# Weights made in three stages a step apart, large transfers on ScalarE's queue, two banks for p6, x's high parts on ScalarE, the opening's sums on GpSimd

## Time and profile before

| | us |
|---|---|
| median of the runs | 2794.37 |
| profiled execution, its own time | 2791.71 |
| its span, first to last instruction | 2789.9 |
| TensorE busy | 2471.3 (89%) |
| VectorE busy | 1668.8 (60%) |
| ScalarE busy | 975.5 (35%) |
| GpSimd busy | 402.0 (14%) |

### The profile page before, as it was taken

One profiled execution on the slowest core, in us unless ns is written; L12 is line 12 of the kernel. 1 busy time (PEld: TensorE's weight loads), 2 busy tenths in 40 slices (PEclk: granted clock), 3 DMA queues, 4 the chain that ended last, 5 costly groups with the idle time before them and its releaser, 6 DMA issues. The chain is left out here.

```text
span 2789.9 us, 30463 instructions
## 1 busy us (share of the span) xinstructions
PE 2471.3 (89%) x11214; PEld 1119.0 (40%) x11214; DVE 1668.8 (60%) x2827; ACT 975.5 (35%) x1247; POOL 402.0 (14%) x296
## 2 busy tenths in 40 slices
PE   2669879787787888999999999999899999999999
PEld 1324334333332333444444444444344444444444
DVE  7676667765676676577878878765543252241341
ACT  6575556544454454444454444111000000001001
POOL 1020101111222221111111111111101001001011
PEclk8789999988898998999999999999999999999999
DMA  6445454545445444855566555431776777686774
GB/s 226 155 147 159 146 187 157 182 137 176 157 165 176 158 167 145 321 196 185 192 211 212 200 177 193 144 107 71 291 317 256 307 274 299 260 323 265 282 311 153
DMA packets 172993, 571.15 MB, mean 205 GB/s; under 512 B 23632, under 2 KB 48896, under 8 KB 155052
## 3 DMA queue, kind: packets, MB, share of 16 engines
q1 hardware_dynamic: 163484, 535.11, 53.1%
q10 hardware_dynamic: 9360, 34.08, 3.9%
HBM read 380.38 MB, written 188.75 MB: 204 GB/s over the span
## 5 line engine op out<-in xcount | busy, mean ns | idle before, releaser
L1512 PE MATMUL ps<-arena 128*128 128x512 f16 x7200 | 1621.8, 388 | 169.5 <-DVE arena L1116 86.5
L1512 PEld LDWEIGHTS ps<-arena 128*128 128x128 f16 x7200 | 715.4, 100 | 1063.4 <-issue 171.7
L1631 PE MATMUL ps<-arena 128*128 128x512 f16 x3696 | 800.4, 380 | 10.4 <-DVE arena L1320 10.4
L822 ACT ACTIVATE arena<-arena,bias_t 128x1024 f32<-128x1024 f32 (+1 forms) x520 | 574.2, 1141 | 33.9 <-DMA arena<-in_dn 13.8
L1631 PEld LDWEIGHTS ps<-arena 128*128 128x128 f16 x3696 | 362.1, 98 | 448.7 <-issue 14.2
L1154 DVE CAST arena<-arena 128x512 f16<-128x512 f32 x364 | 204.6, 574 | 211.7 <-POOL arena L777 71.7
L1157 DVE TENSOR_TENSOR arena<-arena 128x512 f16<-128x512 f32 x364 | 297.3, 829 | 0.0
L767 POOL TENSOR_TENSOR arena<-arena 128x512 f32<-128x512 f32 x52 | 78.3, 1507 | 1138.5 <-DVE arena L1288 952.7
L837 ACT ACTIVATE arena<-arena 128x512 f16<-128x512 f32 x147 | 86.3, 622 | 339.8 <-DVE arena L1084 132.1
L888 ACT ACTIVATE arena<-ps,gate_back 128x512 f32<-128x512 f32 x84 | 57.4, 683 | 381.4 <-PE ps L1512 381.2
L787 POOL TENSOR_TENSOR arena<-arena 128x512 f32<-128x512 f32 x64 | 84.3, 1326 | 699.8 <-DMA arena<-in_xt 574.2
(11 more groups left out here) (106 smaller groups left out, 1245.9 us busy)
## 6 DMA issues: line engine op xcount, KB each, us to landing
isc<-arena SPq DMA_DIRECT2D x308, 256.0 KB, 2.0
arena<-wdsc SPq DMA_DIRECT2D x28, 2816.0 KB, 9.8
arena<-isc SPq DMA_DIRECT2D x28, 2816.0 KB, 16.8
arena<-xnsc SPq DMA_DIRECT2D x48, 1024.0 KB, 16.6
wsc<-arena SPq DMA_DIRECT2D x21, 1792.0 KB, 7.5
arena<-wsc SPq DMA_DIRECT2D x42, 768.0 KB, 5.2
arena<-in_gu ACTq DMA_DIRECT2D x43, 512.0 KB, 4.1
wdsc<-arena SPq DMA_DIRECT2D x77, 256.0 KB, 2.1
```

The source lines that it names most:

```text
L822: a_.activation(buf, src, ACT.Prelu, bias=bias_t[:, i:i + 1], scale=scale, alpha=alpha).then_inc(ramps, 1)
L1512: ins = t_.matmul(ps[:, bank, :], wreg[:, b, w, wa, k, :], xreg[:, j, o, k, xa, :], start=start and (k, wa, xa) == (0, 0, 0), stop=stop an ...
L1631: ins = t_.matmul(ps[:, bank, :], ring_w[b][:, k, wa, g, :], ring_i[b][:, k, xa, :], start=first and (k, wa, xa) == (0, 0, 0), stop=r not ...
```

## The change

- **Weights in three stages.** For weight u + 1: items 0 to 3 in step (u - 1, 1), items 4, 5, 6, 7, 9 in step (u, 0), items 8, 10, 11, 12 in step (u, 1). ScalarE's w_high are grouped as [0, 4, 5] and [1, 3, 6, 2], right behind p1_copy. Of the ramps 10 are in step (u, 0) and 6 in step (u, 1), half ahead of sil_a and half behind it.
- **Queues.** store_w, load_w, load_xb and load_ring are issued by ScalarE, the loads by `reloads` at the start of its step (one after sil_a).
- **Banks.** From step 23 on p6 alternates between banks 6 and 7. The first products of the closing phase wait for their own bank.
- **x jobs.** ScalarE makes the high parts (`x_high`), VectorE only the low parts.
- **Opening.** GpSimd makes all four sums of each early block. The layer norm of tiles 0 to 7 and of tiles 8 to 15 is one group each, with three applies of each on GpSimd; that of 8 to 15 is in slot 3 of step 0, its transposes behind step 0's products, and its evacuations alternate with w_high of weight 1. The later norms are in slot 3, not 5. The first weight and block order on VectorE changes with it.
- **Half tile LAST.** It uses operands 0 and 1 of its buffer, not 2 and 3.

The core of the diff (inner code is shown with less indentation):

```diff
 NEARLY = 8
...
+W_AT[0] = [(1, i) for i in range(13)]
+W_AT[2] = [(2, i) for i in range(4)]
+W_AT[3] = [(2, i) for i in (4, 5, 6, 7, 9, 8, 10, 11, 12)] + [(3, i) for i in range(4)]
 for _s in range(4, 40):
     _u, _j = PASS[_s]
-    W_AT[_s] = (_u + 1, 0, 6) if _j == 0 else (_u + 1, 6, 13)
-RAMP_AT = {0: (1, 4, 16), 1: (2, 0, 12), 2: (2, 12, 16), 3: (3, 0, 16)}
+    if _j == 0:
+        W_AT[_s] = [(_u + 1, i) for i in (4, 5, 6, 7, 9)]
+    else:
+        W_AT[_s] = [(_u + 1, i) for i in (8, 10, 11, 12)] + [(_u + 2, i) for i in range(4) if _u + 2 < LAST or i == 0]
+W_AT[40] = [(LAST, 6)]
+STORE_W_AT = {0: 1, 3: 2, 40: LAST}
+STORE_W_AT.update({_s: PASS[_s][0] + 1 for _s in range(4, 40) if PASS[_s][1]})
+RAMP_AT = {0: (1, 4, 16), 1: (2, 0, 8), 2: (2, 8, 16), 3: (3, 0, 16)}
 for _s in range(4, 40):
     _u, _j = PASS[_s]
     if _u + 2 < NU:
-        RAMP_AT[_s] = (_u + 2, 8 * _j, 8 * _j + 8)
+        RAMP_AT[_s] = (_u + 2, 0, 10) if _j == 0 else (_u + 2, 10, 16)
 NDOWN = 11
 for _i in range(4):
     RAMP_AT[40 + _i] = (NU, 4 * _i, 4 * _i + 4)
...
+W_CUT = {5: [0, 0, 0, 1, 2, 3, 5], 8: [0, 0, 0, 1, 2, 3, 8], 13: [0, 0, 0, 0, 0, 0, 13], 4: [0, 0, 0, 0, 0, 0, 4],
+         9: [0, 0, 0, 0, 0, 0, 9], 1: [0, 0, 0, 1, 1, 1, 1], 0: [0] * 7}
+W_CUT[9], W_CUT[5], W_CUT[6] = [0, 0, 2, 3, 4, 5, 9], [0, 0, 1, 2, 3, 4, 5], [0, 0, 1, 2, 3, 4, 6]
+def p6_bank(s):
+    return 6 if s < 23 else 6 + s % 2
+def p6_before(s):
+    return next((t for t in range(s - 1, -1, -1) if p6_bank(t) == p6_bank(s)), None)
...
         g.tensor_tensor(early_t[:, 1, :], b[:, 0, 1, :], b[:, 0, 0, :], ALU.subtract).then_inc(ep_made, 1)
+        pool.wait_ge(ep_made, 4 * e + 1)
+        g.tensor_tensor(early_t[:, 2, :], b[:, 1, 1, :], early_t[:, 1, :], ALU.subtract).then_inc(ep_made, 1)
+        if e:
+            pool.wait_ge(e_lo, 5 * e - 1)
+        pool.wait_ge(ep_made, 4 * e + 2)
+        g.tensor_tensor(early_t[:, 0, :], b[:, 1, 0, :], early_t[:, 2, :], ALU.subtract).then_inc(ep_made, 1)
         if e:
             pool.wait_ge(e_lo, 5 * e)
         g.tensor_tensor(early_t[:, 3, :], b[:, 1, 1, :], b[:, 0, 1, :], ALU.subtract).then_inc(ep_made, 1)
+    def lnorm_share(tiles):
+        pool.wait_ge(ln_out, tiles[0] // 8 + 1)
+        for tt in tiles:
+            g.tensor_scalar(nat[nat_slot(tt)], nat[nat_slot(tt)], mv[:, tt % 8, 0:1], y[:, 1, tt % 8:tt % 8 + 1],
+                            ALU.subtract, ALU.mult).then_inc(xn_done, 1)
     def sums(c):
...
+        early_sums(e)
+    lnorm_share([13, 14, 15])
+    for e in range(4, NEARLY):
         early_sums(e)
     for c in JOBS:
         sums(c)
...
+    def store_w(u):
+        act.wait_ge(w_lo, w_base(u + 1, 7, 1))
+        b = wbuf(0, u)
+        if u == LAST:
+            act.dma_start(wsc[u, :, 0:2, :, :], wflat[:, b, 0:2, :, :]).then_inc(wst[u % 2], 16)
+        else:
+            act.dma_start(wsc[u, :, :, :, :], wflat[:, b, :, :, :]).then_inc(wst[u % 2], 16)
...
+    def load_w_first(u):
+        load_w(u, 0, 1)
+        load_w(u, 4, 7)
+    def load_w_second(u):
+        load_w(u, 1, 2)
+        load_w(u, 2, 4)
...
+    def reloads(s):
+        h, u, j = STEPS[s]
+        if h == 0:
+            if s == 41:
+                act.wait_ge(prod, prod_at(40, "p5"))
+                load_xb(0, 5)
+                load_xb(0, 6)
+                act.wait_ge(prod, prod_at(39, "p3"))
+                load_w(0, 4, 7)
+                load_w(0, 2, 4)
+            elif s == 42:
+                act.wait_ge(prod, prod_at(41, "r"))
+                act.wait_ge(prod, prod_at(40, "p3"))
+                for o in (0, 4, 2, 3):
+                    load_xb(0, o)
+            elif s == 43:
+                act.wait_ge(prod, prod_at(42, "p5"))
+                load_w_first(1)
+                act.wait_ge(prod, prod_at(41, "p2"))
...
+                load_xb(1, o)
+        elif s == NSTEP + 1:
+            act.wait_ge(prod, prod_at(43, "p2"))
+            load_w(0, 1, 2)
+            load_xb(1, 1)
+        elif s == NSTEP + 3:
+            act.wait_ge(prod, prod_at(s - 1, "p5"))
+            load_w_first(2)
+        elif s == NSTEP + 4:
+            act.wait_ge(prod, prod_at(s - 2, "p3"))
+            load_w_second(2)
+            act.wait_ge(prod, prod_at(s - 1, "p5"))
+            load_w_first(3)
+        elif s == NSTEP + 5:
+            act.wait_ge(prod, prod_at(s - 2, "p3"))
+            load_w_second(3)
+        elif u == 20 or u == LAST:
+            if (u, j) == (LAST, 1):
+                act.wait_ge(prod, prod_at(s - 2, "p2"))
+                load_ring(0)
+        elif u >= 3 and j == 0:
+            act.wait_ge(prod, prod_at(s - 1, "p5"))
+            load_w_first(u + 1)
+        elif u >= 3 and j == 1:
+            act.wait_ge(prod, prod_at(s - 2, "p3"))
+            load_w_second(u + 1)
...
+    def x_high(c, o):
+        if made_before(c, o):
+            act.wait_ge(t_made, 4 * JOB[c] + made_before(c, o))
+        else:
+            act.wait_ge(blk_in, 32 * x_number(c) + 32)
+        n = STAGED[c + (o,)]
+        if n >= NSLOT:
+            act.wait_ge(st_out[n % NSLOT], 16 * (n // NSLOT))
+        a_.activation(dest(c, o)[:, 0, :], operand_of(c, o), ACT.Copy).then_inc(x_hi, 1)
...
-    for s in range(TOTAL + 1):
+    store_w(0)
+    def ramps_of(s, a, b):
+        w, first, end = RAMP_AT.get(s, (0, 0, 0))
+        for n in range(first + (end - first) * a // 4, first + (end - first) * b // 4):
+            ramp(w, n)
+    p1_copy(0)
+    ramps_of(0, 0, 4)
+    for at, ops in ((8, [0]), (10, [4, 5]), (12, [1, 3]), (14, [6, 2])):
+        for tt in (at, at + 1):
+            for hh in (0, 1):
+                evac(tt, hh)
+        for o in ops:
+            w_high(1, o)
+    for e in EARLY_AT[0]:
+        for g in range(5):
+            early_high(e, g)
+    for s in range(1, TOTAL + 1):
+        h, u, j = STEPS[min(s, TOTAL - 1)]
+        if s < TOTAL:
+            reloads(s)
         if s >= 2:
             sil_b(s - 2)
         if half_tile_at(s - 1, "p3"):
             evac(*half_tile_at(s - 1, "p3"))
         if s < TOTAL:
             p1_copy(s)
-        if s == 0:
-            for tt in range(8, 12):
-                for hh in (0, 1):
-                    evac(tt, hh)
-        h, u, j = STEPS[min(s, TOTAL - 1)]
-        wu, w0, w1 = W_AT.get(s, (None, 0, 0))
-        ru, r0, r1 = RAMP_AT.get(s, (None, 0, 0))
-        if 4 <= s < 40 and wu != LAST:
-            for o in ([0], [1, 3])[j]:
-                w_high(wu, o)
+        if 4 <= s < 40 and u + 1 != LAST:
+            for o in ([0, 4, 5], [1, 3, 6, 2])[j]:
+                w_high(u + 1, o)
+        if s in XJOB_AT:
+            for o in (0, 1, 2):
+                x_high(("x",) + XJOB_AT[s], o)
         if half_tile_at(s, "p6"):
             evac(*half_tile_at(s, "p6"))
-        for n in range(r0, r0 + (r1 - r0) // 4):
-            ramp(ru, n)
-        if s == 0:
-            for tt in range(12, 16):
-                for hh in (0, 1):
-                    evac(tt, hh)
+        ramps_of(s, 0, 2)
+        if s in XJOB_AT:
+            for o in (4, 5):
+                x_high(("x",) + XJOB_AT[s], o)
         if half_tile_at(s, "p5"):
             evac(*half_tile_at(s, "p5"))
-        if s:
-            sil_a(s - 1)
+        sil_a(s - 1)
+        if s == 40:
+            w_high_last()
+        elif s == 43:
+            act.wait_ge(prod, prod_at(43, "r"))
+            load_w(0, 0, 1)
+        elif s == NSTEP + 40:
+            load_w(LAST, 0, 1)
+            load_w(LAST, 1, 2)
         if half_tile_at(s, "p2"):
             evac(*half_tile_at(s, "p2"))
...
+                x_high(("x",) + XJOB_AT[s], o)
+        for e in EARLY_AT.get(s, ()):
+            for g in range(5):
+                early_high(e, g)
+        if s == 3:
             for o in W_ORDER:
-                w_high(wu, o)
-        if s == 0:
...
         tp, r = i // 7, i % 7
+        if i == 0:
+            act.wait_ge(prod, len(PRODS))
+        if i + 1 < 28:
+            load_ring(i + 1)
...
-    def lnorm(tiles):
+    def lnorm(tiles, mine):
         m = len(tiles)
+        if tiles[0] >= 8 and m == 8 or tiles[0] == 16:
...
-        for i, tt in enumerate(tiles):
+            if k < 2 or m < 8:
+                step(v_.tensor_tensor(r, r, t, ALU.mult))
+            else:
+                v_.tensor_tensor(r, r, t, ALU.mult).then_inc(ln_out, 1)
+                dve.wait_ge(ln_out, tiles[0] // 8 + 1)
+        for i, tt in enumerate(tiles[:mine]):
             v_.tensor_scalar(nat[nat_slot(tt)], nat[nat_slot(tt)], mv[:, i, 0:1], y[:, 1, i:i + 1],
                              ALU.subtract, ALU.mult).then_inc(xn_done, 1)
...
+                return
             if made_before(c, o):
                 dve.wait_ge(t_made, 4 * JOB[c] + made_before(c, o))
-            elif c[0] == "x":
-                dve.wait_ge(blk_in, 32 * x_number(c) + 32)
             else:
                 s = step_of(c[2] // 2, 2 * c[1] + 1, c[2] % 2)
                 dve.wait_ge(ib_made, s + 1)
```

(56 more changed lines are left out.)

261 lines of the change are left out of this document (76 added, 185 removed).

## The result

The changed kernel takes 2672.18 us (median of 4 runs, 2668.99 to 2672.88) against 2796.60 for the kernel before on the same chip (4 runs): a ratio of 0.9552, 95% interval 0.9535 to 0.9568. The profiled execution spans 2671.1 us at a granted clock of 0.967. The forecast was 2597, so 119 us of span were gained where 196 were expected.

The account below looks back on a forecast made before the run. TensorE bounds the kernel, idling where VectorE is late, notably steps 23 to 38. Gains 87 + 56 + 15 + 38 = 196 take the span from 2789.9 to 2594, time 2597; range 2565 to 2635, wide range 2540 to 2675.

Parts of the forecast that it names:

- (a): Both long stretches: half the gain, as x_high's way is paid in full and bursts hold staging slots; 2668 us, chance 0.16.
- (d): Weights: three stages don't work, w_high still waits for VectorE; casts, norm, opening and queues alone pay; 2656 us, chance 0.12.
- Opening, minus 15 forecast: To the end of step 4: sums and applies move from VectorE to GpSimd, first products end sooner; minus 15 us.
- Steps 7 to 22, minus 56: Later tiles' layer norm: moved to slot 3, it shortens the stall in every fourth step; 386.8 becomes 331, minus 56 us.
- cycle of 82.7: Steps 7 to 22: four steps take 18.1 + 26.6 + 18.1 + 20.0 = 82.7 us, four times.
- Steps 23 to 38, minus 87: Where x's blocks are split: three weight stages and x's highs on ScalarE relieve VectorE; 424.3 becomes 337, minus 87 us.
- x's highs: Steps 23 to 38: seven casts in each of 8 steps leave VectorE, 28 us; new waits of 18 and 8.
- the second block 5 late, four times, 20: Steps 23 to 38: VectorE's wait for each pair's second block, behind the first job's last low and four scale loads.
- balance for VectorE before (421.5 of 424.3): Steps 23 to 38, kernel before: VectorE's busy time plus three waits nearly fills the stretch, so VectorE is the bound.
- Steps 41 to 45, minus 12: Transfers on ScalarE's queue: w_high_last no longer holds step 41; minus 12 of the 17 us over the floor.
- Steps 46 to 88 and the closing phase, minus 26: Transfers leave SP's queue, closing phase asks one bank at a time: minus 9, minus 5 and minus 12 us.
- (c): All steps: DMA issues block ScalarE and slow the kernel; at 3 us a step 2861 us, chance 0.04.

Follow-up runs that it names:

- o2: The changed kernel with all layer-norm applies of the opening and two of the four sums of each early block on VectorE again: 2646.89 us.
- n1: The kernel before with one edit, the norm of two later tiles in slot 3, not 5: 2816.47 us, ratio 1.0090.
- q1: The kernel before with one edit, stores of weights 3 to 19 issued by ScalarE at the end of the next step, not by SP: 2744.02 us.
- x2: The changed kernel with the high parts of x's blocks (steps 22 to 35) on VectorE again: 2665.30 us.
- s1: The changed kernel with weights made in two stages as before, ramps half and half: 2723.75 us.

## Why the prediction was right in sign and 75 us too low

The time lies 3 us inside the wide range (2540 to 2675) and 37 above the forecast's own (2565 to 2635), nearest to rivals (a) and (d), and neither is what happened. The direction was right for the reason given: TensorE idled because VectorE was late, and work and waits taken off its way came back as time. Point by point:

- **Opening, minus 15 forecast, plus 17 measured.** The mis-sized term is GpSimd: an apply taken as 1.9 (bounds 0.7 to 2.6) is 4.4 to 4.9, outside both bounds, and a block 7.5 is 9.9 because the later sums in line take 1.6 to 2.2, not 1.28. "Twice its sum of 512" was a poor upper bound, since it came from another kind of instruction. That the rest of the working stood is shown by o2: its first products end at 81.7 us, forecast "near 81" (95.8 in the changed kernel), and the opening at 213.1 against the 208 forecast.
- **Steps 7 to 22, minus 56, measured minus 46.** The size is near by luck, the cause was wrong. I gave all of it to the norm's place; n1 shows that place alone to cost 23. The largest piece measured is the moved store_w (24, q1), which the prediction mentioned only for blocks; VectorE's 27.0 for staging slots in this stretch, behind the bytes of that store, never entered the sum. The stages bring 12. My cycle of 82.7 held nearly (341.2 / 4 = 85.3) because it was written for a VectorE without that wait, without saying what removes it.
- **Steps 23 to 38, minus 87, measured minus 67.** Three stages did what the text says: the waits of ScalarE's weight high parts come to 18.7 (227.9 before), the silu of B costs VectorE 8.2. Taken out, they are worth 43 here; put in alone, the moved store is worth 21. x's highs were counted as 28 of VectorE's casts saved against some 26 of new waits; x2, where VectorE is busy only 12.8 longer (282.9 and 270.1), has them as a loss of 8. The term that failed is "the second block 5 late, four times, 20": it is 7.7 late on average (30.6 / 4), and it doesn't hold VectorE alone but ScalarE, with the silu of A behind it, which the prediction never put in that order. Its balance for VectorE before (421.5 of 424.3) closed in part by chance: it counts 10 us of a wait for a block (11.5, ended at 647.8) that lie ahead of the stretch, and leaves out 9.0 for a sum of GpSimd (L774).
- **Steps 41 to 45, minus 12, measured plus 5.** The 5.0 at step 41 went as forecast; 12.8 at step 42 came. The prediction took SP's waits away and did not count the bytes, nor that SP's order had kept x's loads behind the stage stores. The rule of the Trainium skill that it cited against itself (DMA: Bandwidth & Descriptors, "Issuing engines are not separate DMA queues") says that all issuers' transfers interleave on the same engines. The trace agrees: stores on SP's queue land after a median of 10.3 us beside loads on ScalarE's, and 8.5 with a quarter of x's bytes. It should have been priced here, not left to rival (a).
- **Steps 46 to 88 and the closing phase, minus 26, measured minus 31.** As forecast. Rival (c) is false: issues on ScalarE's queue in steps 41 to 43 take 0.33 to 1.3 us each, and of all 243 in the changed kernel two exceed 1 us.
- **Two banks: nothing**, as forecast.
- **Rival (d), the stages don't take hold:** false, s1 loses 51.6 us without them. **Rival (a):** its two mechanisms exist (x_high's way, bursts that hold slots), but the halves of the gain in the long stretches were not lost: 112 of 143 came.
- The misses add up: 32 in the opening, 10, 20 and 17 in the three stretches, 2.4 in steps 5 and 6, less 5 from step 46 on: 77 unrounded, all that is missing.
